# First layer: each expert's float32 product replaced by three float32r products on halves

## The reference

```
x  = L0_attn_x                                   # 8 batches x 512 tokens x 128
xn = layernorm(x)
x  = x + attention(xn) + experts(xn)
gate_probs = softmax(xn @ gate_w.T + gate_b)     # 8 true and 2 null experts
weights, selected = top_k(gate_probs, 2)
combine_w = weights of the true experts among them, scaled to sum 1
expert_out = einsum('td,edh->teh', xn, expert_w) + expert_b
experts = einsum('te,teh->th', combine_w, expert_out)
```

## Time and profile before

| what | value |
|---|---|
| median of 3 runs | 1955.6 us |
| the profiled execution's own time | 1957.46 us |
| its span, first to last instruction | 1955.7 us |
| PE busy | 1781.2 us (91%) |
| DVE busy | 989.1 us (51%) |
| ACT busy | 843.1 us (43%) |
| POOL busy | 238.6 us (12%) |
| `layer0_mix`, from its first to its last PE instruction | 37.03 to about 462.4 us of the span |
| L741, expert products: 128 matmul instructions for 64 products | 72.8 us |
| mean granted TensorE clock | 0.956 |

### The profile page before, as it was taken

How to read it: one execution, slowest core, us unless ns; L and a number is a source line. 1 busy time by engine, 2 the same in 40 slices (tenths; PEclk the granted TensorE clock), 3 DMA queues, 4 the chain that set the end, 5 groups by cost and what they waited for, 6 DMA issues and landing times. The chain is left out here.

```text
span 1955.7 us, 22682 instructions
## 1 busy us (share of the span) xinstructions
PE 1781.2 (91%) x8518; PEld 1002.1 (51%) x8518; DVE 989.1 (51%) x1612; ACT 843.1 (43%) x1025; POOL 238.6 (12%) x210
## 2 busy tenths in 40 slices
PE   7589999998788989999999999999999979999995
PEld 4222222224453436766767586758576734444442
DVE  3454444444774434444444443434444446677765
ACT  4467777775333324333333243333333343444441
POOL 1000000000561001010101010000001022233322
PEclk8699999998879989999999999999999989999998
DMA  1232222122006620000000000000000010000001
GB/s 71 38 52 44 44 44 44 44 44 113 1 1 141 148 59 0 1 1 1 1 1 1 1 1 1 1 1 1 1 1 0 2 52 1 0 0 0 0 0 43
DMA packets 19116, 48.90 MB, mean 25 GB/s; under 512 B 784, under 2 KB 1552, under 8 KB 18000
## 3 DMA queue, kind: packets, MB, share of 16 engines
q1 hardware_dynamic: 19024, 47.63, 10.0%
HBM read 45.14 MB, written 2.36 MB: 24 GB/s over the span
## 5 line engine op out<-in xcount | busy, mean ns | idle before, releaser
L494 ACT ACTIVATE probs<-ps_ring 128x1024 f32<-128x1024 f32 x256 | 246.0, 1023 | 124.2 <-PE ps_ring L708 121.5
L1733 PEld LDWEIGHTS ps_o<-v,probs 128*128 128x128 f32 x2048 | 236.5, 192 | 34.7 <-issue 31.4
L1733 PE MATMUL ps_o<-v,probs 128*128 128x129 f32 x2048 | 250.8, 279 | 1.8 <-ACT probs L1476 1.2
L1476 ACT ACTIVATE probs<-ps_ring 128x1024 f32<-128x1024 f32 x128 | 127.0, 1024 | 242.1 <-PE ps_ring L1714 242.0
L1546 DVE TENSOR_REDUCE negmax<-ps_o 128x2 f32<-128x1024 f32 x64 | 78.5, 1226 | 167.0 <-PE ps_o L1689 167.0
L722 PE MATMUL ps_o<-probs,v 128*32 128x512 f32 x1024 | 139.3, 618 | 13.1 <-DVE o_sb L545 13.1
L1468 ACT ACTIVATE probs<-ps_ring,pack 128x512 f32<-128x512 f32 x64 | 40.5, 685 | 180.9 <-PE ps_ring L1662 105.5
L1662 PE MATMUL ps_ring<-probs,pack 128*128 128x512 f32 x256 | 117.2, 602 | 0.0
L1559 DVE RECIPROCAL rden<-ps_o 128x2 f32<-128x2 f32 x128 | 21.5, 168 | 178.7 <-PE ps_o L1733 178.7
L1926 POOL TENSOR_TENSOR rs<-r,state 128x512 f32<-128x512 f32 x64 | 81.6, 1275 | 206.6 <-DVE state L2018 202.9
L708 PEld LDWEIGHTS ps_ring<-q_stack,k_stack 32*128 32x128 f32 x512 | 31.6, 187 | 124.9 <-issue 100.6
(11 more groups left out here) (363 smaller groups left out, 3304.9 us busy)
## 6 DMA issues: line engine op xcount, KB each, us to landing
cwb<-combine_by_expert SPq DMA_DIRECT2D x8, 2048.0 KB
score<-score_by_expert SPq DMA_DIRECT2D x7, 2048.0 KB, 13.8
pack<-pack_dram SPq DMA_DIRECT2D x1, 2560.0 KB, 13.3
pack<-pack_dram SPq DMA_DIRECT2D x1, 2443.0 KB, 9.4
x<-x_in SPq DMA_DIRECT2D x2, 1024.0 KB, 6.2
out<-x SPq DMA_DIRECT2D x1, 2048.0 KB, 6.3
score<-score_by_expert SPq DMA_DIRECT2D x1, 1536.0 KB, 13.5
pack<-pack_dram SPq DMA_DIRECT2D x1, 1451.0 KB, 7.6
```

Source lines behind the costliest of these rows:

```text
L494: nc.scalar.activation(probs[n % 3][:, 2 * half:2 * half + 2, :], ps, ACT.Exp, scale=float(HD0) ** -0.5).then_inc(read, 1)
L1476: nc.scalar.activation(probs[:, n % 2, m, :, :], ps, ACT.Exp).then_inc(read, 1)
L1733: last = nc.tensor.matmul(ps_o[:, i, k * (D + 1):(k + 1) * (D + 1)], probs[:, (b * PAIRS + p) % 2, m, j, queries], v[:, m, h, :], start=(m ...
```

## The change

Each expert product becomes three float32r products. DVE still forms the weighted tokens in float32, drains, and then writes them rounded to float32r (`xe_high`); POOL subtracts that from the float32 value (`xe_low`). The expert matrices are split the same way once, at the start: DVE rounds (`expert_high`), POOL subtracts (`expert_low`). PE waits for `xe_low`, no longer for `xe`. DVE's reuse of a buffer waits for POOL as well as for PE.

```diff
-        xe = sb("xe", [P, 3, T])
+        xe, xe_high, xe_low = (sb(n, [P, 3, T]) for n in ("xe", "xe_high", "xe_low"))
+        wide = E0_TRUE * P
+        expert_high, expert_low = sb("expert0_high", [P, wide]), sb("expert0_low", [P, wide])
...
         def _(pool):
...
+            pool.wait_ge(expert_high_ready, 1)
+            nc.gpsimd.tensor_tensor(single(expert_low[:, :]), w["expert0"], expert_high[:, :], ALU.subtract).then_inc(expert_ready, 1)
+
+            def rest(b):
+                for n in range(b * E0_TRUE, (b + 1) * E0_TRUE):
+                    pool.wait_ge(xe_ready, n + 1)
+                    nc.gpsimd.tensor_tensor(single(xe_low[:, n % 3, :]), xe[:, n % 3, :], xe_high[:, n % 3, :], ALU.subtract
+                                            ).then_inc(xe_low_ready, 1)
+
             for b in range(B):
                 was_read(pool, ("qk", b))
                 nc.gpsimd.tensor_tensor(sq[:, :, :], qk[:, :, :], qk[:, :, :], ALU.mult).then_inc(squared, 1)
+                if b:
+                    rest(b - 1)
+            rest(B - 1)
...
             nc.vector.tensor_tensor(bound[:, 0:8], w["qs_row"], w["ks_row"], ALU.mult)
+            nc.vector.tensor_copy(single(expert_high[:, :]), w["expert0"]).then_inc(expert_high_ready, 1)
             nc.vector.tensor_copy(single(sel[:, :, :]), w["select"].rearrange("p (s c) -> p s c", c=P)).then_inc(sel_ready, 1)
...
                     dve.wait_ge(xe_used, n - 2)
-                nc.vector.tensor_tensor(xe[:, n % 3, :], xn[:, at(b)], cwb[:, e, :], ALU.mult).then_inc(xe_ready, 1)
+                    dve.wait_ge(xe_low_ready, n - 2)
+                nc.vector.tensor_tensor(xe[:, n % 3, :], xn[:, at(b)], cwb[:, e, :], ALU.mult)
+                dve.drain()
+                nc.vector.tensor_copy(single(xe_high[:, n % 3, :]), xe[:, n % 3, :]).then_inc(xe_ready, 1)
...
                 n = b * E0_TRUE + e
-                pe.wait_ge(xe_ready, n + 1)
-                nc.tensor.matmul(ps_y[:, :], w["expert0"][:, e * P:(e + 1) * P], xe[:, n % 3, :],
-                                 start=(e == 0), stop=False).then_inc(xe_used, 1)
+                pe.wait_ge(xe_low_ready, n + 1)
+                if n == 0:
+                    pe.wait_ge(expert_ready, 1)
+                of = slice(e * P, (e + 1) * P)
+                split_products(nc, ps_y[:, :], (expert_high[:, of], expert_low[:, of]), (xe_high[:, n % 3, :], xe_low[:, n % 3, :]),
+                               e == 0, False).then_inc(xe_used, 1)
```

More of the change, by code:

```diff
@@ L415, in layer0_mix @@
         xe_ready, xe_used = sem("xe_ready"), sem("xe_used")
+        xe_low_ready, expert_high_ready, expert_ready = sem("xe_low_ready"), sem("expert_high_ready"), sem("expert_ready")
         y_done, x_added = sem("y_done"), sem("x_added")
```

## The result

The changed kernel takes 2029.6 us, the median of 4 runs (2022.71 to 2042.61), against 1955.9 for the kernel before beside it (1954.66 to 1958.32): a ratio of 1.038 [1.032, 1.044]. It is slower by 73.7 us, outside the predicted range of 1960 to 1988, on the predicted side. The profiled execution took 2023.91 us, its span 2022.1, at a mean granted clock of 0.927 instead of 0.956. Medians and ranges in this document leave out four executions of 2258 to 3777 us, which were disturbed.

What follows compares the result with a forecast made beforehand. PE was taken to bound the layer, with ACT setting the pace in sets 8 to 12 of a batch. The terms 6.6 + 0 + 3.5 + 3.0 + 4.0 = 17.1 us took 1955.6 to 1972.7; range 1960 to 1988.

Steps and rivals of the forecast that it cites:

- the predicted side: Whole kernel: slower than the kernel before by over 0.2%, chance 0.88.
- The products: PE's split product takes 0.78 us, not 1.05: saves 0.27 each, 1.45 per batch in batches 1 to 6.
- inner load: Rival, on PE: the split product's two inner weight loads are paid, so it costs 1.16 us; total 1990; chance 0.02.
- DVE and POOL exclude each other: DVE's SBUF products and casts and POOL's instructions exclude each other; POOL waits about 0.5 us before expert 6.
- The wait at expert 6: Set 14, before expert 6: PE's wait of 0.52 us grows by 2.3 us (1.8 to 2.8).
- Batches 1 to 6 without the clock: Saving -1.45, wait +2.3, DVE's used-up free time +0.25: +1.1 us each, 6.6 in all (2.4 to 10.2).
- Batch 7: No RMS steps in this batch, so all eight savings count: -2.16 + 2.3 = 0 us (-0.5 to 1.5).
- Batch 0 and the start: Batch 0: experts start later, +3.5 us (1 to 7.5). Start: expert-matrix split delays first copies, +3.0 (0.7 to 4.0).
- The clock: PE's clock falls behind the new gap at expert 6 in three of seven batches: +4.0 us (0 to 10).
- falls after every new gap and stays down: Rival on PE's clock: it falls after each new gap, staying down over the next sets; 1983 to 1992; chance 0.12.
- The rival without exclusion: DVE and POOL don't exclude each other for these forms; wait at expert 6 is 1.8; total 1959; chance 0.09.

Runs made afterwards that it cites:

- e11: The change with earlier weighing, a later split of the expert matrices, and `copy_o(b-1,3)` ahead of the next q and k copy: 1935.3 us, 0.990.
- e12: The kernel before with only `copy_o(b-1,3)` moved ahead of the copy of the next q and k on DVE: 1939.5 us, 0.991.
- e4: The change, but DVE makes the token subtraction itself and POOL's loop and the waits for it go: 1990.0 us, 1.015.
- e9: The change with two float32 products with zeros on PE ahead of the wait for expert 6 in batches 1 to 7: 1980.1 us, 1.012.
- e8: The kernel before with five unused copies on DVE between `copy_o(b,2)` and weigh 6 in batches 1 to 7: 2002.6 us.
- e10: The change with two float32 products with zeros on PE behind expert 6 in batches 1 to 7: 2012.7 us, 1.028.

## Why the prediction was wrong

*The products.* No inner load is paid, but the saving is 0.15 us each, not 0.27: 0.78 was read where triple follows triple. Eight give 1.2 us; e11 against e12 has 1.05 per batch, where 1.45 was predicted, and 48.6 - 48.0 = 0.6 from batch 7's first `times_v` to the second layer, not 2.16.

*DVE and POOL exclude each other.* Right for the new instructions: where they meet, a cast takes 1.33 us instead of 0.43, and a subtraction 1.64 instead of 1.28. That the instructions need not meet to bring the clock down, e4 shows.

*The wait at expert 6.* Right: 2.69 to 2.86 us, so 2.2 to 2.3 added.

*Batches 1 to 6 without the clock.* Predicted +1.1 each; with the gap filled, batches without a fall take 48.5 and 48.7, before 46.9 to 47.2: +1.6, half a us more than predicted, about the products' smaller saving (1.45 - 1.05). The upper end of this term should be 9.6, not 10.2, by its own numbers (2.8 - 1.45 + 0.25 = 1.6 each).

*Batch 7.* Predicted 0; with the gap filled 50.7 us to the second layer against 48.6: +2.1. The saving is smaller by 1 us, and PE waits for expert 3 there too, 0.88 us in the change, which the prediction had not.

*Batch 0 and the start.* Predicted +3.5 and +3.0. Batch 0: 70.5 - 65.9 = +4.6, with waits of 2.91 us for expert 3 and 2.04 for expert 4; 26.1 us at half clock lie in it against 20.5 before, so a part of the 4.6 is the clock's. The start: PE's first projection comes at 33.5 to 34.1 us in some executions and at 36.8 to 37.0 in others, with the change or without. Like against like, the way from there to the first score is 26.6 to 26.7 against 22.7 to 22.9, and 25.3 to 25.7 against 21.3: +3.7 to +4.4. DVE's copy of q and k stands at 41.09, not near 43.5, for that reason alone: it is 7.4 us behind the first projection, where it was 3.8 (3.6 us later, 2.7 predicted).

*The clock.* **This is the step that failed**: "I count three of seven: +4.0 (0 to 10, where each of seven falls and some last longer)". Filling the gap took 49.4 us away. The clock fell at expert 6 in all seven batches. The term had one price for a fall, 1.3 us, from the only kind of fall that it had looked at, behind the 2.0 us wait of set 2, where the clock is back after 3.4 us. Behind a wait at expert 6 it stayed down for up to 20.5 us, and such a batch took 58.2 us where one without a fall took 48.5 (e9). The rival "falls after every new gap and stays down" had the mechanism, but it, too, was priced with 14 us. The rival without exclusion took a shorter gap to be "short enough for the clock"; e4's 1.75 us was not.

Without the clock at expert 6 the terms measured here give 6 x 1.6 + 2.1 + 4.6 + 3.7 to 4.4 = 20 to 21 us where 13.1 were predicted; the run with the filled gap is 21.5 us above the kernel before (1980.1 - 1958.6). So some 50 of the 73.7 us are the clock's, against 4.0 predicted, and some 7 of the error of 57 (2029.6 - 1972.7) come from the other terms.

Left open: why the same wait is followed by 3.4 us in batches 1 and 2, by 20.5 later, and in one batch of e8 by nothing; and what ends a stretch where no work of 128x128 stands.

## What to carry to other kernels

Before an edit lengthens a wait of PE, ask what PE does behind it and price the wait with the half clock that may follow, not with its own length: here 2.2 us of added wait made a batch up to 10 us longer than the same batch with the wait filled. A producer's chain that has become longer (a cast, then another engine's subtraction) belongs earlier in the order and needs buffers for it; with that the same work cost nothing. And look for the waits that are there already: moving one copy ahead of another on DVE was worth 1%, about all that the best version gained.

## What the runs showed of the hardware

A busy PE can stay at half clock: 17.10 of 17.10 us busy at 0.50 in e4. What follows a wait isn't told by its length: 1.75 us at expert 6 were followed by 17.1 us at half clock in five batches (e4), 2.0 us in set 2 by 3.4 us or none in every profile, 3.02 us at expert 6 once by none (e8). In the long stretches PE ran products of 32 rows or of 32 columns for the most part (60 of the 70 from 334.90 to 355.40 in the change), with some full ones between; with 3.6 us of 128x128 float32 products put behind expert 6 the full clock was back after 6.8 us in each of seven batches (e10). That these products are the reason is a guess, since short stretches ended without any. More work on PE made the kernel faster, by 49.4 us ahead of the wait and 16.9 us behind it, though it computes nothing.
